# Layer 0's experts: every expert for every token, or tokens grouped by expert in 39 blocks

## The reference

```
logits = xf @ Wg.T + bg
probs = softmax(logits)
tp, ti = top_k(probs, 2)
tp = tp / (sum(tp) + 1e-8)
w = sum(one_hot(ti, 8) * tp[..., None], axis=1)
h = gelu(einsum('td,efd->tef', xf, W1) + b1)
y = einsum('tef,edf->ted', h, W2) + b2
out = einsum('ted,te->td', y, w)
```

## Time and profile before

| | |
|---|---|
| median of 3 runs (lowest to highest) | 2430.76 us (2423.88 to 2432.16) |
| the profiled execution: its time, its span | 2425.25 us, 2423.5 us |
| TensorE busy over the span | 2001.8 us, 83% |
| VectorE | 1824.0 us, 75% |
| ScalarE | 1393.0 us, 57% |
| GpSimd | 527.5 us, 22% |
| mean granted clock of TensorE | 0.906 |
| moved by DMA | 54.94 MB, 23 GB/s |

### The profile page before, as it was taken

One profiled execution on the slowest core, in us unless ns is written; L12 is line 12 of the kernel. 1 busy time (PEld: TensorE's weight loads), 2 busy tenths in 40 slices (PEclk: granted clock), 3 DMA queues, 4 the chain that ended last, 5 costly groups with the idle time before them and its releaser, 6 DMA issues. The chain is left out here.

```text
span 2423.5 us, 36959 instructions
## 1 busy us (share of the span) xinstructions
PE 2001.8 (83%) x12584; PEld 1173.2 (48%) x12584; DVE 1824.0 (75%) x3749; ACT 1393.0 (57%) x3262; POOL 527.5 (22%) x516
## 2 busy tenths in 40 slices
PE   7898998989737999999459999999999842458887
PEld 3477786768536777767211222222222232435554
DVE  5554554545577988989789999999999267389987
ACT  3265665656535555555314888888888841244444
POOL 3022222222371211212500000000000040443322
PEclk9899999999858999999767999999999966679999
DMA  3011111111010000000030101010100000010001
GB/s 119 9 34 27 34 34 27 34 27 34 18 49 28 1 0 0 0 0 0 31 106 15 30 15 29 16 29 16 29 16 15 1 1 2 4 40 0 0 0 35
DMA packets 48315, 54.94 MB, mean 23 GB/s; under 512 B 9976, under 2 KB 35728, under 8 KB 48016
## 3 DMA queue, kind: packets, MB, share of 16 engines
q1 hardware_dynamic: 47556, 51.99, 7.7%
q10 hardware_dynamic: 588, 0.81, 0.1%
HBM read 27.88 MB, written 8.78 MB: 15 GB/s over the span
## 5 line engine op out<-in xcount | busy, mean ns | idle before, releaser
L1621 ACT ACTIVATE probs<-s_ps 128x512 f32<-128x512 f32 x1024 | 534.0, 603 | 140.8 <-PE s_ps L1552 140.6
L1639 DVE TENSOR_REDUCE q_max<-s_ps 128x1 f32<-128x1024 f32 x512 | 599.2, 1219 | 11.8 <-PE s_ps L1531 5.5
L1531 PE MATMUL s_ps<-k_stack,q_stack 64*128 64x512 bf16 x1024 | 358.0, 404 | 21.4 <-PEq L86 10.8
L1158 DVE TENSOR_TENSOR moe_hid_lo<-moe_hid,moe_hid_hi 128x512 fp32r<-128x512 f32 x384 | 330.9, 862 | 13.1
L1552 PE MATMUL s_ps<-q_stack,k_stack 64*128 64x512 bf16 x1024 | 314.9, 384 | 21.0 <-ACT probs L1621 14.5
L1566 PE MATMUL o_ps<-probs,v_aug 128*32 128x512 f32 x2048 | 273.6, 606 | 0.7 <-ACT probs L1621 0.7
L1126 POOL TENSOR_TENSOR nat<-nat,moe_ym 128x512 f32 x112 | 157.6, 1407 | 533.1 <-DVE moe_ym L1139 533.1
L1107 ACT ACTIVATE moe_hid<-moe_hps,moe_b 128x512 f32<-128x512 f32 x256 | 175.9, 688 | 154.0 <-PE moe_hps L1069 86.2
L1552 PEld LDWEIGHTS s_ps<-q_stack,k_stack 64*128 64x128 bf16 x1024 | 78.2, 94 | 336.4 <-ACT probs L1621 285.2
L734 ACT ACTIVATE probs<-s_biased,s_min 128x128 f32<-128x128 f32 x512 | 199.6, 395 | 44.8 <-DVE s_min L772 44.8
L799 POOL TENSOR_TENSOR probs<-probs,p_rsum 128x512 f32<-128x512 f32 x128 | 133.1, 1040 | 374.9 <-DVE p_rsum L778 374.9
(11 more groups left out here) (289 smaller groups left out, 3444.4 us busy)
## 6 DMA issues: line engine op xcount, KB each, us to landing
v_shift<-v_tiles SPq DMA_DIRECT2D x32, 256.0 KB, 3.1
v_shift<-v_tiles SPq DMA_DIRECT2D x32, 224.0 KB, 3.6
qk_parts_dram<-qk_parts SPq DMA_DIRECT2D x16, 384.0 KB, 2.4
q_stack<-qk_parts_dram SPq DMA_DIRECT2D x180, 32.0 KB
k_stack<-qk_parts_dram SPq DMA_DIRECT2D x180, 32.0 KB
x<-in_L_attn_x SPq DMA_DIRECT2D x4, 512.0 KB, 7.2
rt_raw<-in_L_ffn_W1T SPq DMA_DIRECT2D x8, 256.0 KB, 3.3
rt_raw<-in_L_ffn_W2T SPq DMA_DIRECT2D x8, 256.0 KB, 3.1
```

Of the source, the lines that this page charges most:

```text
L1158: v.tensor_tensor(hid[1][:, s % 2, f, :], hf[:, n % 3, :], hid[0][:, s % 2, f, :].bitcast(F32), ALU.subtract).then_inc(hid_lo, 1)
L1531: mm = nc.tensor.matmul(s1[u % 2][:, c * CH:(c + 1) * CH], qs[head_rows(m), quad % 4, j, qt * P:(qt + 1) * P], ks[head_rows(m), quad % 4, ...
L1621: nc.scalar.activation(pr[:, k % 2, HEADS[pos], :], bank_of("exp", n)[:], ACT.Exp).then_inc(sm["exp"], 1)
L1639: v.tensor_reduce(mx[:, quad % 2, col:col + 1], s1[u % 2][:], AX.X, ALU.max).then_inc(sm["maxed"], 1)
```

## The change

The routing moves into the double norm, by batches of 1024 tokens: logits (TensorE), softmax, ranks, the two chosen experts and their weights (VectorE, `choose`), then `prefix`: two matmuls that count, for each tile, how many tokens chose an expert before each token; `place` makes of this a row number in a DRAM tensor `moe_rows` of 34560 rows, in which each expert has a span of its own. GpSimd scatters the normalised tokens there, each to two rows, by one indirect DMA for each tile and choice (64 in all). `tabulate` makes a table of expert and first row for 39 blocks of 256 rows: 32 full blocks' worth of pairs and up to 7 more for spans that end inside a block. There are always 39, whatever the tokens chose.

`block_stage` handles the blocks in order: SP reads expert and row from the table into registers, loads the 256 rows (128 KB) and the expert's weights and biases (578 KB), and stores 256 result rows over the rows it read. TensorE turns the rows, multiplies them with W1 and W2 in plain fp32, without split parts; ScalarE makes the gelu of 4 times 128x256. `gather_stage` fetches each token's two result rows by 64 more indirect DMAs, and VectorE, for each four tiles, weighs them (4 instructions of 128x128), adds (4), gates and adds to x (2 of 128x512). `residual`, in VectorE's queue of the block stage, adds the gated `nat`.

GpSimd fills `moe_rows` (17.7 MB) with zeros by 10 DMAs in the window attention's set-up, between `fill`'s buffers and line 489, and an empty block after the attention waits for them. `routing_stage` and `expert_stage` stay for layer 1. The weights reach the kernel as one array `L0_ffn_blocks` of (8, 128, 1156). New routines that the cut diff leaves out: buffers, `logits`, `shift_logits` (3 steps), `exponentials` (one ScalarE instruction a batch), `tabulate` (15 steps), `residual`.

```diff
@@ -39,6 +39,13 @@
 E = 8
 F0, F1 = 512, 256
 TOPK_EPS = 1e-8
+BR = 256
+SPAN = B * T
+NBK = 2 * B * T // BR + E - 1
+ROWS = E * SPAN + (E - 1) * BR
+ZR = 3
+STEPS_OF = T * B // BR
...
+                for b in range(B + 3 + 2 * (M is not None)):
+                    if M and 4 <= b < B + 4:
+                        M.shift_logits(dve, b - 4)
...
+                    if 3 <= b < B + 3:
                         N2.normalised_odd(dve, b - 3)
+                    if M and 4 <= b < B + 4:
+                        M.choose(dve, b - 4)
+                    if M and b >= 5:
+                        M.place(dve, b - 5)
+                if M:
+                    M.tabulate(dve)
...
+                if M:
+                    for b in range(B):
+                        M.scatter(pool, N2, b)
+                    M.wait_scattered(pool)
...
+                for b in range(B + (M is not None)):
+                    if b < B:
+                        N2.turn(pe, banks, b)
+                        if M:
+                            M.logits(pe, N2, b)
                     if M and b >= 1:
-                        M.logits(nc, K, pe, N2, b - 1)
-                if M:
-                    M.logits(nc, K, pe, N2, B - 1)
+                        M.prefix(pe, b - 1)
...
+            nc.gpsimd.memset(zero[:], 0.0).then_inc(filled, 1)
+            pool.wait_ge(filled, 4)
+            rows = K.moe_rows.rearrange("(p r) d -> p (r d)", p=P)
+            for n in range(ROWS // P // ZR // 9):
+                part = rows[:, 9 * n * ZR * D:9 * (n + 1) * ZR * D].rearrange("p (k z) -> p k z", k=9)
+                pool.dma_start(part, bc(zero[:], 1, 9)).then_inc(cleared, 16)
...
+        with nc.Block() as block:
+            @block.sync
+            def _(sp):
+                sp.wait_ge(cleared, 16 * (ROWS // P // ZR // 9))
...
+    def step(self, dve, ins):
+        self.n += 1
+        ins.then_inc(self.chain, 1)
+        dve.wait_ge(self.chain, self.n)
...
+    def choose(self, dve, b):
+        v, ts = self.nc.vector, slice(b * TPB, (b + 1) * TPB)
+        step, pb, rank, hot = self.step, self.pb[:, ts], self.rank[:, ts], self.hot[:, :, ts]
+        dve.wait_ge(self.exped, b + 1)
+        step(dve, v.tensor_reduce(self.sm[:, ts], self.ex[:, ts], AX.X, ALU.add))
+        step(dve, v.reciprocal(self.rs[:, ts], self.sm[:, ts]))
+        step(dve, v.tensor_tensor(pb, self.ex[:, ts], bc(self.rs[:, ts], 2, E), ALU.mult))
...
+        v.tensor_tensor(g4, over, own, ALU.is_gt)
+        step(dve, v.tensor_tensor(e4, over, own, ALU.is_equal))
+        step(dve, v.tensor_tensor(self.eq[:], self.eq[:], bc(self.low[:], 1, TPB), ALU.mult))
+        step(dve, v.tensor_tensor(self.gt[:], self.gt[:], self.eq[:], ALU.add))
+        step(dve, v.tensor_reduce(rank, g4, AX.X, ALU.add))
+        v.tensor_scalar(self.chosen[:, ts], rank, 2.0, None, ALU.is_lt).then_inc(self.chose, 1)
...
+    def place(self, dve, b):
+        v, step = self.nc.vector, self.step
+        dve.wait_ge(self.prefixed, b + 1)
+        total = self.cp[b % 2][:, 1, 0:TPB * E].rearrange("p (t e) -> p t e", e=E)
+        for t in range(TPB):
+            k = b * TPB + t
+            step(dve, v.tensor_tensor(self.cum[:, k + 1, :], total[:, t, :], self.cum[:, k, :], ALU.add))
+        ts = slice(b * TPB, (b + 1) * TPB)
+        step(dve, v.tensor_tensor(self.slots[:], self.cp[b % 2][:, 0, 0:TPB * E].rearrange("p (t e) -> p t e", e=E),
+                                  self.cum[:, ts, :], ALU.add))
+        step(dve, v.tensor_tensor(self.picked[:], bc(self.slots[:], 1, 2), self.hot[:, :, ts], ALU.mult))
+        step(dve, v.tensor_reduce(self.place_f[:], self.picked[:], AX.X, ALU.add))
+        v.tensor_copy(self.slot[:, :, ts], self.place_f[:]).then_inc(self.placed, 1)
...
+    def scatter(self, pool, N, b):
+        pool.wait_ge(self.placed, b + 1)
+        N.wait_normalised(pool, (b + 1) * TPB)
+        for t in range(b * TPB, (b + 1) * TPB):
+            for c in range(2):
+                self.nc.gpsimd.indirect_dma_start(
+                    self.K.moe_rows, bass.IndirectOffsetOnAxis(ap=self.slot[:, c, t:t + 1], axis=0), N.hat[:, t, :], None
+                ).then_inc(self.scattered, 16)
...
+                rows = {}
+                for j in range(NBK + 2):
+                    if j < NBK:
+                        e = nc.sync.value_load(M.table[0:1, 0, j:j + 1], min_val=0, max_val=E - 1)
+                        rows[j] = nc.sync.value_load(M.table[0:1, 1, j:j + 1], min_val=0, max_val=ROWS - BR)
+                        if j >= XB:
+                            sp.wait_ge(turned, j - XB + 1)
+                        sp.dma_start(xi[:, j % XB], K.moe_rows[bass.ds(rows[j], BR), :].rearrange("(p a) d -> p a d", a=H)
+                                     ).then_inc(x_in[j % XB], 16)
+                        if j >= WBUF:
+                            sp.wait_ge(y_out, j - WBUF + 1)
+                        sp.dma_start(wb[:, j % WBUF, :], M.blocks[bass.ds(e, 1)].rearrange("e p w -> p (e w)")
+                                     ).then_inc(w_in[j % WBUF], 16)
+                    if j >= 2:
+                        k = j - 2
+                        sp.wait_ge(y_out, k + 1)
+                        sp.dma_start(K.moe_rows[bass.ds(rows.pop(k), BR), :].rearrange("(p a) d -> p a d", a=H),
+                                     ys[:, k % YB]).then_inc(stored[k % YB], 16)
...
+                def turn(j):
+                    pe.wait_ge(x_in[j % XB], 16 * (j // XB + 1))
+                    if j >= 2:
+                        pe.wait_ge(x_out, j - 1)
+                    for a in range(H):
+                        m = nc.tensor.transpose(xp[j % 2][:, a * P:(a + 1) * P], xi[:, j % XB, a, :], K.ident[:])
+                    m.then_inc(turned, 1)
+                def hidden(j):
+                    pe.wait_ge(w_in[j % WBUF], 16 * (j // WBUF + 1))
+                    pe.wait_ge(x_out, j + 1)
+                    for f in range(FC):
+                        n = FC * j + f
+                        if n >= 4:
+                            pe.wait_ge(g_out, n - 3)
+                        nc.tensor.matmul(hp[n % 4][:, 0:BR], wb[:, j % WBUF, f * P:(f + 1) * P], xT[:, j % 2, :],
+                                         start=True, stop=True).then_inc(h_mm, 1)
+                def out_rows(j):
+                    pe.wait_ge(g_out, FC * (j + 1))
+                    if j >= 2:
+                        pe.wait_ge(y_out, j - 1)
+                    for a in range(H):
+                        for f in range(FC):
+                            m = nc.tensor.matmul(yp[j % 2][:, a * P:(a + 1) * P], hid[:, j % 2, f, a * P:(a + 1) * P],
+                                                 wb[:, j % WBUF, F + f * D:F + (f + 1) * D],
+                                                 start=(f == 0), stop=(f == FC - 1))
+                    m.then_inc(y_mm, 1)
+                turn(0)
+                for j in range(NBK + 1):
+                    if j + 1 < NBK:
+                        turn(j + 1)
+                    if j < NBK:
+                        hidden(j)
+                    if j >= 1:
+                        out_rows(j - 1)
...
+                def tokens_out(j):
+                    dve.wait_ge(turned, j + 1)
+                    if j >= 2:
+                        dve.wait_ge(h_mm, FC * (j - 1))
+                    v.tensor_scalar(xT[:, j % 2, :], xp[j % 2][:, 0:BR], M.affine[:, 0:1], M.affine[:, 1:2],
+                                    ALU.mult, ALU.add).then_inc(x_out, 1)
+                def rows_out(j):
+                    dve.wait_ge(y_mm, j + 1)
+                    if j >= YB:
+                        dve.wait_ge(stored[j % YB], 16 * (j // YB))
+                    y = yp[j % 2][:, 0:BR].rearrange("p (a d) -> p a d", a=H)
+                    if M.biased:
+                        r = v.tensor_tensor(ys[:, j % YB], y, bc(wb[:, j % WBUF, 2 * F + FC:], 1, H), ALU.add)
+                    else:
+                        r = v.tensor_copy(ys[:, j % YB], y)
+                    r.then_inc(y_out, 1)
...
+                tokens_out(0)
+                for j in range(NBK + 1):
+                    if j + 1 < NBK:
+                        tokens_out(j + 1)
+                    if j >= 1:
+                        rows_out(j - 1)
+                    if 2 <= j < NCH + 2:
+                        residual(j - 2)
...
+            def _(pool):
+                for t in range(NT):
+                    for c in range(2):
+                        nc.gpsimd.indirect_dma_start(
+                            yg[:, t, c, :], None, K.moe_rows, bass.IndirectOffsetOnAxis(ap=M.slot[:, c, t:t + 1], axis=0)
+                        ).then_inc(got[t // CPT], 16)
...
-            M = Experts(K, "moe0", F0, A["L0_ffn_W1T"], A["L0_ffn_W2T"], A["L0_ffn_b1c"], A["L0_ffn_WgT"],
-                        A["L0_ffn_bg"], st)
```

(74 more changed lines are left out.)

194 lines of the change are left out of this document (190 added, 4 removed).

## The result

The changed kernel took 2546.39 us (median of 4 runs, 2544.23 to 2547.39) against 2429.56 us before in the same session (4 runs): a ratio of 1.0483, 95% interval 1.0463 to 1.0503. It is slower by 117 us; the forecast was 2590, or +161, with a range from 2450 to 2740.

What follows compares the result with a forecast made beforehand. Stages run serially, the old expert loop at TensorE's limit; new blocks would wait on SP's in-order queue and a throttled clock. Difference -430 + 128 c + 39 T: end 1324 against 1162.8, +161 us, forecast 2590, range 2450 to 2740.

Steps and rivals of the forecast that it cites:

- Start of the scatter: After norm and routing: first batch's places near 712 us, one more empty block 1.8, so scattering begins at 714.
- The scatter: GpSimd's 64 indirect DMAs, one per token tile and choice, at 1.2 us each: 77 us.
- c: Price of one indirect DMA on GpSimd, in scatter and gather: 1.2 us, estimated between plain issues and large GpSimd instructions.
- From the scatter's end to the first load: Between scatter and block stage: last landing 2.2 us, stage boundary 1.8, two register reads 0.8 each.
- The blocks: Block stage: 39 blocks, each a 5.3 us gap from SP's queue order plus a 5.9 us partly throttled burst: 437 us.
- T: Period of one block in the block stage: 11.2 us, bounds 8.0 to 14.1.
- The gather: After the blocks: 64 indirect DMAs on GpSimd 77 us, landing 2.2, last four tiles on VectorE 3.6: 83 us.
- Full clock is kept: Block stage: TensorE's clock stays full since bursts are dense; period 9.0 us, +75 us, 2503; chance 12%.
- Cheap requests: GpSimd and SP addressing near plain issue cost, 0.6 us per indirect DMA, period 8.8: -10 us, 2418; chance 10%.
- The loads are hidden: Block stage: queue order misread or SP's wait met early; TensorE paces at 4.5 us: -100 us, 2328; chance 3%.
- Expensive GpSimd: Scatter and gather: 2.0 us per indirect DMA, +263 us, 2690, or 2740 with period 12.5; chance 20%.
- VectorE holds GpSimd back: Scatter's address work waits until VectorE's routing ends at 745, starting 31 us late: 2621; chance 10%.

Runs made afterwards that it cites:

- the experiment: The two register reads of the next block moved ahead of the store's wait on SyncE, against the changed kernel: 2501.73 us.
- the third experiment: 16 unused matmuls per block added on TensorE in the gap before the next block's turning, against the changed kernel: 2483.66 us.
- the order mended: Store three turns behind, register reads ahead of its wait and clearing by SyncE, all together, against the changed kernel: 2317.57 us, 0.9555 of before.

## Why the prediction was right, and by how much it was off

The sign and the mechanism held. The terms were not all that near, and their errors partly cancelled. Step by step:

- **Start of the scatter.** Forecast 714, measured 715.78. VectorE took up the first logits at 690.23 instead of 688. All 2.1 us of the double norm's later start (655.97 against 653.9) are in it; the prediction put the clearing at nothing, and its 10.35 us on GpSimd's queue are the cause: with them on SyncE the norm started 2.2 us or more ahead of every start with them on GpSimd. That this shortens the whole is not shown.
- **The scatter.** c = 1.2 forecast, 1.26 measured; 81.0 us instead of 77. The grounds for 1.2 were partly wrong: I argued from an address for each row, and the price hardly depends on the rows. That it came so near is luck in part.
- **From the scatter's end to the first load.** 5.6 us in the sum (landing 2.2, boundary 1.8, two reads 1.6), 10.3 measured. This term was too small. Its part for reads and issue was right: from the first instruction of the next stage (805.49) to the load 1.6 us pass. Landing and boundary, 4.0 in the sum, took 8.7. The cause is open; the number of rows and, for all but 1.5 us, the waiting engine are ruled out.
- **The blocks.** T = 11.2 forecast, 9.84 measured: 39 x 1.36 = 53 us. This is the term that was mis-sized, and the reason for the difference of 40 us. From the first load to the first gather the sum had 444.4 us and the trace 391.7. Of the 1.36 the gap holds 1.1: 4.2 instead of 5.3, just under the low end of 4.3 that I had given it. The end of the last matmul cost 0.04 and not 0.17, the copy and its hops 0.45 and not 0.5, the store's issue 0.36 and not 0.45, the reads 1.33 after the store's issue (1.14 by the experiment) and not 1.6, issue to turning 2.13 and not 2.6, since I had added 0.4 of hops and queueing to a landing that already held them. The burst holds the rest: 5.6 instead of 5.9.
- **The gather.** 83 forecast, 85.4 measured.

Sum against the forecast's 161: +1.8, +4.0, +4.7, -52.7, +2.4 makes 121, the measured difference of the profiled executions. So the total missed by less than the blocks did, because the other four terms were each too small, by 12.9 us together.

One sign that I had named didn't come: GpSimd's wait before `woT_gated`, 47.2 us in the earlier trace rows, was to stay near 47. It fell to 38.0, and still the instruction began at 105.62 instead of 102.10:

```profile
105.62 2.34 POOL L828 TENSOR_TENSOR woT_gated<-woT,mod_rows 128x1024 f32<-128x1024 f32 x1 [38.01 <-POOLq L93]
```

So the wait did not hide GpSimd's issuing of the clearing in full. With the clearing on SyncE the instruction began at 101.52.

- *Full clock is kept* (T = 9.0, 2503) did not happen, though the shorter gap brought T near it. Had the clock been kept with this gap, the third experiment says 2484.
- *Cheap requests* would have needed 128 c + 39 T below 430; with c = 1.26 and T = 9.84 it was 545. Its gap of 4.3 us did come, its cheap GpSimd didn't: the 128 indirect DMAs followed one another every 1.26 us on average. The experiment with fewer rows shows that smaller requests wouldn't have helped.
- *The loads are hidden* was put at 2328, and that state is what the kernels with the later store and with the stores on GpSimd built: 2330 and 2319. The nearness is luck in part. That rival took T = 4.5 and called it TensorE's pace, although the prediction's own price for TensorE's work was 3.7, which is right: 3.73. The 0.8 too much for each block made up for the terms that were too small.
- *Expensive GpSimd* (c = 2.0): no, 1.26. *VectorE holds GpSimd back*: no. The scatter starts at 715.8 while VectorE works on until 743.8, when the table is made; the pitch is 1.29 us up to there and 1.26 after. The Trainium skill (SBUF — State Buffer, "SBUF: two separate sides") lets certain VectorE instructions lock GpSimd out, one instruction at a time. This trace shows no such wait of note beside these instructions.

The gain that was on offer, 401.5 - 145 = 256 us, was nearly all there: with the stores on GpSimd the stage takes 160.1 us from the first load (809.2) to the first gather (969.3), 241 less than the 401.5 of before. The changed kernel spent 216 to 229 of it in the gap and the slow clock, and it took 177 us for scatter and gather on top; with the order mended, the kernel is 108 us faster than before.

## What to carry to other kernels

In an in-order queue that both stores results and loads inputs, a store that waits for the newest result puts the next load behind it, and the four input buffers here didn't help; let the store lag one turn more, or give it to another queue, and compute the period again before judging the new algorithm. A gap of 4 us per turn costs twice: once as itself, and once in the clock of the burst behind it. Before sorting rows through DRAM, count the indirect DMAs, not the rows: 128 of them are 160 us here, and with a quarter or half of the rows in each hardly less.

## What the runs showed of the hardware that I had not expected

- An indirect DMA holds GpSimd about 0.86 us plus 0.8 ns a row in the scatter (0.4 ns in the gather), and the next starts 0.30 us later; a plain 128 KB store from GpSimd 0.54 us, while each of the ten plain clearing transfers of 1728 KB took 1.03 (10.35 us together).
- A read of one table entry into a register costs SyncE 0.28 us for the load and 0.15 for what follows it, 0.57 in all on the path.
- After writes issued by GpSimd the next stage is slow to start: from the end of the last issue to the first instruction of the next stage 8.7 us in the changed kernel (796.8 to 805.5), 7.3 where SyncE waits for the landings in GpSimd's place (797.6 to 804.8), and 6.5 with the stores on GpSimd (962.8 to 969.3). With the stores on SyncE the whole way from the last copy to the next stage was 3.5. The cause is open.
- 592 matmuls that nobody needs, put where TensorE idled, made the kernel 62.7 us faster.
